# Moving the low halves of the softmax weights, the value split of the first attention turn and the transposes of the last one

## The reference

```python
q = rope(rmsnorm(x @ Wq)); k = rope(rmsnorm(x @ Wk)); v = x @ Wv        # 32 query heads, 8 key heads, D = 128
k_all = concat([k_cache[block_table], k]); v_all = concat([v_cache[block_table], v])   # 512 + 128 keys
scores = where(valid, q @ k_all.T * SCALE, -1e30)
o = softmax(scores) @ v_all
x = x + o.reshape(bsz, seqlen, HQ * D) @ Wo.T
```

## Time and profile before

| what | value |
|---|---|
| median of 3 runs (range) | 1334.36 us (1333.95 to 1335.92) |
| profiled execution | 1333.57 us, span 1332.0 us |
| mean granted TensorE clock | 0.992 of full |
| busy: PE / DVE / ACT / POOL | 1297.4 / 972.5 / 779.8 / 756.7 us |
| chain that ended last, by engine | PE 79%, DVE 6%, ACT 4%, issue 4%, POOL 2%, SPq 2% |

### The profile page before, as it was taken

How to read it: one execution, slowest core, us unless ns; L and a number is a source line. 1 busy time by engine, 2 the same in 40 slices (tenths; PEclk the granted TensorE clock), 3 DMA queues, 4 the chain that set the end, 5 groups by cost and what they waited for, 6 DMA issues and landing times.

```text
span 1332.0 us, 25952 instructions
## 1 busy us (share of the span) xinstructions
PE 1297.4 (97%) x6728; PEld 1102.7 (83%) x6728; DVE 972.5 (73%) x2500; ACT 779.8 (59%) x1829; POOL 756.7 (57%) x778
## 2 busy tenths in 40 slices
PE   8999999997999999999999999999999999999997
PEld 8888888886888888788888878888888787888886
DVE  5532344978778877978777788888777878777883
ACT  5731334455566667576666666666566666656663
POOL 3100000257666668776666686766667876666662
PEclk9999999998999999999999999999999999999998
DMA  7321214176555557756555577555557665555533
GB/s 259 130 63 48 71 48 128 52 261 185 121 123 122 125 127 199 182 124 136 127 132 128 141 186 188 121 134 139 131 120 182 178 159 116 121 122 122 122 90 79
DMA packets 314845, 178.01 MB, mean 134 GB/s; under 512 B 260752, under 2 KB 279568, under 8 KB 314512
## 3 DMA queue, kind: packets, MB, share of 16 engines
q1 hardware_dynamic: 296128, 126.88, 39.9%
q0 software_dynamic: 11264, 32.77, 9.8%
q10 hardware_dynamic: 7376, 17.45, 4.0%
HBM read 118.15 MB, written 16.91 MB: 101 GB/s over the span
## 4 chain that ended last, share of the span: by engine, by line
PE 79%; DVE 6%; ACT 4%; issue 4%; POOL 2%; SPq 2%; DMA 1%; ACTq 0%; DVEq 0%; POOLq 0%
PE bank L1555 15%; PE tail L1593 15%; PE wide L1623 12%; PE tail L1657 11%; PE wide L455 4%; PE wide L1587 4%; PE wide L531 3%; PE bank L1576 3%; PE bank L455 2%; PE tail L455 2%; PE wide L583 2%; DVE parts L1968 1%; PE bank L531 1%; ACT prT L1758 1%; POOL wq1T L1303 1%
## 5 line engine op out<-in xcount | busy, mean ns | idle before, releaser
L1593 PE MATMUL tail<-prT,vt 128*128 128x512 f32 x960 | 266.3, 416 | 8.9 <-POOL prT L1349 2.8
L1593 PEld LDWEIGHTS tail<-prT,vt 128*128 128x128 f32 x960 | 173.8, 193 | 55.5 <-DVE prT L1957 12.5
L1286 POOL TENSOR_TENSOR tick<-tick 128x1 f32<-128x1 f32 x254 | 55.8, 220 | 270.6 <-PE tail L1593 91.6
L1657 PE MATMUL tail<-woT,oT 128*128 128x512 f32 x768 | 179.7, 390 | 0.8 <-DVE oT L2008 0.8
L1657 PEld LDWEIGHTS tail<-woT,oT 128*128 128x128 f32 x768 | 144.1, 188 | 31.1 <-DVE oT L2008 1.2
L1623 PE MATMUL wide<-kT,qT 128*128 128x320 f32 x512 | 158.8, 310 | 2.0 <-DVE mx L1984 1.5
L1623 PE MATMUL wide<-kT_low,qT 128*128 128x320 f32 x512 | 158.4, 309 | 0.0
L1623 PE MATMUL wide<-kT,qT_low 128*128 128x320 f32 x512 | 158.1, 309 | 0.0
L1786 ACT ACTIVATE pr<-pr,nm,q_scale 128x640 f32<-128x640 f32 x128 | 118.0, 922 | 42.7 <-DVE nm L1987 42.2
L1786 ACT ACTIVATE raw<-raw,nm,q_scale 128x640 f32<-128x640 f32 x124 | 114.7, 925 | 44.7 <-DVE nm L1987 43.5
L1340 POOL TENSOR_TENSOR parts<-raw,parts 128x1280 f16<-128x1280 f32 x50 | 132.4, 2647 | 7.3
(11 more groups left out here) (280 smaller groups left out, 2912.4 us busy)
## 6 DMA issues: line engine op xcount, KB each, us to landing
w_ring<-pair_weights SPq DMA_DIRECT2D x80, 256.0 KB, 4.3
k_raw<-k_pages SPq DMA_DIRECT2D x512, 32.0 KB, 1.7
v_raw<-v_pages SPq DMA_DIRECT2D x512, 32.0 KB, 2.8
spread<-one_over_denominators ACTq DMA_DIRECT2D x32, 512.0 KB, 4.6
xTb<-x_transposed POOLq DMA_DIRECT2D x31, 512.0 KB, 4.2
rope<-rope_tables SPq DMA_DIRECT2D x31, 256.0 KB, 2.8
out<-y POOLq DMA_DIRECT2D x31, 256.0 KB, 4.9
w_raw<-w_gate_up SPq DMA_DIRECT2D x10, 512.0 KB, 3.3
```

The lines of the kernel that those rows point to most:

```text
L1286: nc.gpsimd.tensor_tensor(tick[:, 2:3], tick[:, 1:2], tick[:, 1:2], ALU.add).then_inc(s_carry, 1)
L1593: last = nc.tensor.matmul(tail[g][:, :], vt[v_part][:, j, g * D:(g + 1) * D], prT[p_part][:, :, j, :], start=(j == v_part == p_part == 0), ...
L1657: last = nc.tensor.matmul(place[:, :], oT[:, g, o_part, (h % REP) * S:(h % REP + 1) * S], woT[w_part][:, h, :], start=(h == o_part == w_pa ...
```

## The change

Five edits. (1) In the first turn GpSimd splits the values before it casts the two halves, and the low part of chunk 14 moves behind the halves. (2) In the first turn and in the six weight turns VectorE makes all four rests behind the last mask; before, two stood behind the sixth mask and two behind the eighth. (3) In the last turn with a front (pair 3, sample 7) the rest of the second half goes from GpSimd to VectorE, behind the last mask. (4) In the last turn TensorE makes the transposes of the second key head's weights ahead of its wait for s_tl; then come all high sums and all low sums. (5) For that, ScalarE's copies of them wait for the high sums (new semaphore s_ph), and VectorE's low parts for the low sums (s_pv), since they overwrite what the sums read.

```diff
--- before.py
+++ after.py
@@ -1131,6 +1131,7 @@
     qT = place(205824, "qT", [P, G, REP * S], F32R)
 
     s_xt = sem("xTb_loaded")
+    s_ph = sem("last_high_sums_done")
     s_ropel = sem("rope_loaded")
     s_high = sem("keys_and_queries_high_part_ready")
     s_k = sem("cached_keys_loaded")
@@ -1385,14 +1386,14 @@
                 rest_low(3)
                 pool.wait_ge(s_init[0], 16 * BLK)
                 pool.wait_ge(s_step, u * NSTEP + MASKED)
-                low_weights(own, 3 * KT, 3 * KT + 3)
+                low_weights(own, 3 * KT, 3 * KT + 2)
                 for i in range(2):
                     pool.wait_ge(m_full[i], B // 2)
                 pool.wait_ge(s_xlast, 16 * (B // 4))
-                halve(u, n, 0, True, False)
-                split_values(u, n + 1, True)
-                halve(u, n + 2, 1, True, False)
-                low_weights(own, 3 * KT + 3, 4 * KT)
+                split_values(u, n, True)
+                for k in range(2):
+                    halve(u, n + 1 + k, k, True, False)
+                low_weights(own, 3 * KT + 2, 4 * KT)
             else:
                 split_values(u, n, not extra)
                 if extra == "next":
@@ -1404,7 +1405,7 @@
                     low_weights(own, 2 * KT, 2 * KT + 2)
                 elif extra == "out":
                     low_weights(own, 4 * KT + 1, 4 * KT + 3)
-                halve(u, n + 2, 1, False, not extra)
+                halve(u, n + 2, 1, False, not extra and then_x is not None)
                 if extra == "next":
                     low_weights(own, 2 * KT + 2, 3 * KT)
                 elif extra == "out":
@@ -1662,6 +1663,10 @@
                 pe.wait_ge(s_wlo, chunks_done(pair, 0) if isinstance(b, int) and b < 2 else chunks_done(pair, NCHUNK))
                 output(tail[1], w, 0, REP)
                 output(tail[1], w, REP, REP).then_inc(s_y, 1)
+            if back and not front:
+                for w in range(2):
+                    probs_wide(1, w)
+                transposes(0, probs_of(1, JT - 1))
             if back:
                 pe.wait_ge(s_tl, u * 2 + 2)
             if front:
@@ -1673,23 +1678,28 @@
                     pe.wait_ge(s_th[k], u + 1)
                 pe.wait_ge(s_vs, u + 1 + FIRST)
                 pe.wait_ge(s_o, u * G + FIRST)
-                sums(0, range(JT), (0, 1), 0)
-                sums(0, (0, 1), (0,), 1)
-                probs_wide(1, 0)
+                highs = sums(0, range(JT), (0, 1), 0)
+                if front:
+                    sums(0, (0, 1), (0,), 1)
+                    probs_wide(1, 0)
+                else:
+                    highs.then_inc(s_ph, 1)
+                    sums(0, range(JT), (0,), 1).then_inc(s_pv, 1)
             if front:
                 if not back:
                     rest.fourth_quarter()
                 pe.wait_ge(s_rope, n * G + 2 + FIRST)
                 transposes(0, [ra[:, REP + i, :] for i in range(G)])
-            if back:
+            if back and front:
                 sums(0, (2, 3), (0,), 1)
                 probs_wide(1, 1)
             if front:
                 transposes(1, [ra[:, REP + G + i, :] for i in range(REP)])
                 rotated = full[1].value()
-            if back:
+            if back and front:
                 sums(0, (JT - 1,), (0,), 1).then_inc(s_pv, 1)
                 transposes(0, probs_of(1, JT - 1))
+            if back:
                 pe.wait_ge(s_yadd, u + FIRST)
                 values(1, 0)
                 values(1, 1)
@@ -1755,6 +1765,8 @@
 
             def high_probs(w):
                 act.wait_ge(t_full[w], u + 1)
+                if not front:
+                    act.wait_ge(s_ph, 1)
                 ac.copy(prT[0][:, :, 2 * w:2 * w + 2, :].rearrange("p h j q -> p j h q"),
                         wide[w][:, :].rearrange("p (j h q) -> p j h q", j=2, h=REP)).then_inc(s_phi, 1)
 
@@ -1952,6 +1964,8 @@
 
             def low_probs(w):
 
+                if not front:
+                    dve.wait_ge(s_pv, u * G + 1 + FIRST)
                 dve.wait_ge(s_phi, u * 3 + w + 1)
                 low, high_part = (t[:, :, 2 * w:2 * w + 2, :].rearrange("p h j q -> p j h q") for t in (prT[1], prT[0]))
                 v.tensor_tensor(low, wide[w][:, :].rearrange("p (j h q) -> p j h q", j=2, h=REP), high_part, ALU.subtract).then_inc(t_free[w], 1)
@@ -2068,9 +2082,8 @@
                         rest.low_x(h)
                     if not back and h in (2, 4):
                         rest.token(h + 3)
-                    if (extra or not back) and h in (REP + 1, HP - 1):
-                        for i in range(HALF):
-                            rest_of((h - REP - 1) // 2 * HALF + i)
+                for h in range(0 if extra or not back else REP if ahead else HALF, REP):
+                    rest_of(h)
                 assert at.n == NSTEP, at.n
         dve.wait_ge(s_keyno, 3)
         turns(dve, turn)
```

## The result

| | before | after |
|---|---|---|
| median (range, runs) | 1334.36 us (1331.67 to 1335.92, 5) | 1342.00 us (1340.47 to 1342.37, 5) |
| profiled execution, span | 1333.57, 1332.0 us | 1342.08, 1340.1 us |
| busy: PE / DVE / ACT / POOL | 1297.4 / 972.5 / 779.8 / 756.7 us | 1299.9 / 972.9 / 780.3 / 749.9 us |

The forecast of 1336.0 and its range to 1340.0 were both too low.

A forecast was written before the change was run, and what follows sets the result against it. TensorE, busy 97%, was taken as the bound, its idle gaps mainly in six weight turns. Terms 2.3 + 2.3 + 0.8 + 0.9 - 4.9 = +1.4 us, put on the median and rounded for risks: 1336.0 us, range 1330.5 to 1340.

The forecast's parts named there:

- The out turns, +2.3 and +0.8 for the clock: Three turns loading output weights: later rests hold SP's transpose queue, +2.3 us; one extra clock fall at half price, +0.8.
- the clock falls in both early out turns: Rival: clock falls there and stays low through the first turn's sums; +5.0 us, 1339.4 us, chance 0.2.
- The last turn, -4.9: Last turn: transposes fill TensorE's gap, sums start earlier without the low clock, output starts at 1317.95, not 1322.92: -4.9 us.
- the case without the clock: Last turn gains only -2.0 us without the clock's part; as a rival +4.3, 1338.7 us, chance 0.12.
- The next turns, +0.9: Three turns loading the next pair's projections: three rests still precede chunk 11's subtraction, TensorE +0.3 us later each, +0.9.
- They take turns: VectorE rests and GpSimd operations alternate on the shared port: rest 0.7 us, cast 1.25, weight subtraction 1.26.
- The first turn, +2.3: First turn: rests end at 316.0 and sums start 1.7 us late, plus 0.6 us for the low clock: +2.3.
- The faster rival: Port free when the rests come, rests 0.81 us beside GpSimd's casts: -8.7 us, half of it 1329.5 us; chance 0.16.

The follow-up runs named there:

- the transposes' order: Changed kernel with SyncE issuing both casts' transposes before both rests' in each pair's first out turn: 1340.06 us, 1.0041; repeated 1338.73 us, 1.0030.
- the memset: Changed kernel with one VectorE memset of 128x384 elements ahead of the four rests of the next turns: 1342.12 us, 1.0062.

## Why the prediction was wrong

- **The out turns, +2.3 and +0.8 for the clock: this step failed.** The queue was seen rightly (three transposes 1.6 us apart behind the last mask), but sized for the best race. I let the first two rests meet no GpSimd operation in between (the second ending at 603.9, 0.7 us ahead of the output product, which starts at 604.6). In the first out turn VectorE's key mask stood behind a GpSimd subtraction (1.60 us instead of 0.54) and GpSimd's values ran 0.9 us late with it, its last weight subtraction fell between the two rests (1.91 us for the second), and that ended 0.14 us behind the output product: the gap became 3.2 us, not 2.1. Of the 18 out turns with late rests in the old order of transposes, the second rest ended 0.5 to 0.7 us ahead of the output product in five, with gaps of 2.3 to 2.9 us; in the other thirteen it ended between 0.12 ahead and 0.15 behind, with gaps of 2.9 to 4.9 us. And the clock was priced at half a fall in three turns, though my own showed one behind 2.04 us; it fell behind 16 of 18, against 7 of 24 before, 1.8 falls more in a run: 3.1 us for the 0.8 taken, which leaves 3.7 of the 6.8 us for the waits that I put at 2.3. The rival "the clock falls in both early out turns" (1339.4 us) had the mechanism; even it ended low, because it kept the other sizes. Shown by the late rests alone in these turns, whose gaps are those of the changed kernel and whose times, without the clock's part, are 3.7 and 4.4 us over; and by the transposes' order: turning it took the gap from 3.25 to 1.57 + 0.39 us, 4.8 us off the changed kernel, and 2.2 and 2.9 us off the waits of the late rests alone.
- **The last turn, -4.9: right in mechanism, priced from an unlucky execution.** In the profile I read it took 21.43 us; over nine profiles the old form means 19.84, and runs from 18.52 to 21.43 as the clock falls or not. The new form took 16.57 to 16.64 us in seven profiles, and 17.10 without the half rest. Two old-form profiles without a fall there took 18.52 and 18.58 us. My 2.0 for the case without the clock and 4.9 for the case with it were near the two ends; the means differ by 3.2. Taking one end as the term, in a kernel whose runs I compared by medians, cost 1.7 us.
- **The next turns, +0.9: the sum was 1.8, and not by the step I gave.** By the means most of the loss is in the first next turn, where the first rest was held for 4.5 us in 3 of 4 profiles without the memset. The waits on chunks 10 and 11 did not grow by it, they shrank (from 2.5 us together to 0.8); what came late were the rests, and the last landing with them. Without the clock's part the three turns cost 2.6 (1.5) us alone, and by the changed kernels with and without them 2.3 or, less the memsets, 1.3. "They take turns" was my reading of rows that all took turns; the rival case, in which GpSimd's whole queue goes first, was not among the bounds.
- **The first turn, +2.3: right**, +2.0 over the profiles; rests ended at 315.66 (316.0 said), sums started at 324.87 (324.7).
- **The faster rival** (rests of 0.81 us beside GpSimd's casts) is out: rests took up to 1.9 us each where GpSimd worked, four of them 6.26 us in the first turn (309.40 to 315.66).

Adding the corrections, 3.7 for the out turns, 0.9, 1.7 and -0.3, to +1.4 gives +7.4 us, against +7.6 and +9.1 measured.

In short, the waits I had summed to +2.9 us (1.7 first turn, 2.3 out, 0.9 next, -2.0 last) and measured +5.2 (1.8); the clock, which I had giving back 1.5 us in all, took 3.4 (1.5).

What stays open: the late rests alone in the out turns measured +3.1 and +5.1, where their places say +6.8. Most of the difference is in the clock: those runs lost -0.3 (1.5) and +1.0 (1.2) us to it and not 3.1, and in both profiles the last turn, which had a fall in all seven others with its old form, had none. Whether the one follows from the other is not shown. Of the waits in the out turns the order of the transposes explains 2.2 to 2.9 us of some 4; the remaining 1.5 stay with the late rests in either order. What decides in the first next turn whether GpSimd or the waiting rest goes next is not settled.

The version that beats the kernel before is the one that keeps only the last turn's edits and the half rest: 0.9979 (0.9959 to 0.9998) and 0.9981 (0.9961 to 1.0000), some 2.7 us, of which 1.6 to 2.0 are waits and the rest is the clock's.

## What to carry to other kernels

Where an engine's queue issues transfers in a fixed order, moving one producer later delays every finished product behind it: find what is already waiting in that queue, and turn its order with the edit. Where the granted clock of every run is listed, split a small difference by it before calling it nothing. Price a gap with the clock that follows it, a fall each time a trace of the same kernel shows one behind a gap of that size. And before taking a place's length from one profiled execution, ask whether the clock was down in it: here one turn varied by 3 us in the same form, more than most edits are worth.

## What the runs showed of the hardware

- **A waiting VectorE instruction can be passed over.** A two-input subtraction on VectorE and a GpSimd operation exclude each other; the Trainium skill's page "SBUF — State Buffer", section "Who interferes with whom", has it so, and the rows agree. In most places they took turns (1.9 us for a rest of 0.81). But of twelve first rests that started 0.04 to 0.10 us behind the start of GpSimd's tick (a one-element operation ahead of its cast), three, at 0.07 and 0.08 us, lasted 4.48 or 4.49 us, until a cast and two weight subtractions had passed them. The other nine took 0.8 to 2.0 us. Two rests of the old order took 7.57 us once. Moved some 0.4 us later, into the cast, none took over 1.9 us in three turns; but nine of the twelve unmoved ones were short too, so it is not shown that the arrival decides.
- **The low clock is not decided by the one gap.** It came behind gaps of 2.2 us, and of 0.87 + 0.81 us in one out turn of the old form, and stayed away behind one of 3.06 and one of 3.46 us (both with late rests in the out turns). The Trainium skill's page "TensorE: Matmul & The Clock Gate", section "HAM oscillation", has longer gaps as the cause; these runs show falls behind shorter ones. The low stretches behind these gaps lasted 3.4 us, once 6.8, and cost about half of that. The kernel before scatters by 0.8%: 35 runs on one chip lay between 1328.95 and 1340.04 us, and their times follow their granted clock with a correlation of -0.97.
